# DLRM tower on one core: a first id block laid out per partition, one-hot units of 513 columns for three more steps, a spare lookup bank and a reordered tail

## What is computed

```python
e = jnp.stack([tbl_f[ids[:, f]] for f in range(26)], axis=1)     # (2048, 26, 128)
combined = jnp.concatenate([e, r_dense_x[:, None, :]], axis=1)   # 27 rows a sample
z = jnp.einsum('bfd,bgd->bfg', combined, combined)[:, TRIU_I, TRIU_J]   # 351 pairs
h = jnp.concatenate([z, r_dense_x], axis=1)                      # 479 wide
h = jnp.maximum(h @ W_top1 + b_top1, 0.0)                        # 512
h = jnp.maximum(h @ W_top2 + b_top2, 0.0)                        # 256
y = h @ W_top3                                                   # 1
```

## Time and profile before

| what | us |
|---|---|
| median of 3 runs | 358.75 |
| the profiled execution itself | 359.39 |
| its span, first to last instruction | 357.7 |
| TensorE (PE) busy | 336.0 |
| VectorE (DVE) busy | 238.4 |
| GpSimd (POOL) busy | 250.0 |
| ScalarE (ACT) busy | 178.3 |
| TensorE not busy in the last stretch, 320 to 358 | 7.6 (38.0 less 30.4 busy) |

### The profile page before, as it was taken

How to read it: one execution, slowest core, us unless ns; L and a number is a source line. 1 busy time by engine, 2 the same in 40 slices (tenths; PEclk the granted TensorE clock), 3 DMA queues, 4 the chain that set the end, 5 groups by cost and what they waited for, 6 DMA issues and landing times.

```text
span 357.7 us, 12506 instructions
## 1 busy us (share of the span) xinstructions
PE 336.0 (94%) x5576; PEld 278.2 (78%) x5576; DVE 238.4 (67%) x440; ACT 178.3 (50%) x238; POOL 250.0 (70%) x265
## 2 busy tenths in 40 slices
PE   7998899797999999999999999999999999998976
PEld 7787777676878788877888788787888788977864
DVE  2999989774378856787468784787587793430322
ACT  3898534381617634283535735176344827363412
POOL 6788777777777777777777777777777777777000
PEclk9999999998999999999999999999999999999999
DMA  6988683333343343335253334333443322222000
GB/s 222 369 238 268 171 245 87 87 82 99 71 111 84 86 99 100 85 81 118 64 121 96 82 99 93 88 83 88 100 97 88 94 55 56 66 54 55 24 2 3
DMA packets 19657, 37.67 MB, mean 105 GB/s; under 512 B 5557, under 2 KB 8501, under 8 KB 19604
## 3 DMA queue, kind: packets, MB, share of 16 engines
q1 hardware_dynamic: 11412, 20.09, 20.0%
q0 software_dynamic: 8192, 16.79, 18.6%
HBM read 36.85 MB, written 0.01 MB: 103 GB/s over the span
## 4 chain that ended last, share of the span: by engine, by line
PE 72%; DVE 19%; issue 4%; ACT 2%; DMA 2%; SPq 0%; DVEq 0%; ACTq 0%
PE ps_lk L638 26%; DVE onehot L336 15%; PE ps_gram L664 14%; PE ps_tr L649 8%; PE ps_zt L691 7%; PE ps_mlp L691 6%; PE ps_zt L698 3%; PE ps_mlp L698 3%; DVE table L347 3%; PE ps_lk L711 2%; DMA ids<-in_ids_onehot 2%; PE ps_zt L678 1%; PE ps_lk L726 1%; ACT ids L440 0%; ACT xt L460 0%
## 5 line engine op out<-in xcount | busy, mean ns | idle before, releaser
L294 POOL DMA_INDIRECT rows<-in_tbl,gather_ids x256 | 248.7, 971 | 79.7 <-issue 76.2
L336 DVE TENSOR_SCALAR onehot<-ids 128x513 fp32r<-128x513 f32 (+3 forms) x328 | 179.9, 621 | 40.1 <-PE ps_lk L638 24.0
L638 PE MATMUL ps_lk<-onehot,table 128*128 128x512 f32 (+1 forms) x720 | 160.8, 375 | 4.5 <-DVE onehot L336 1.8
L638 PEld LDWEIGHTS ps_lk<-onehot,table 128*128 128x128 f32 x720 | 121.2, 188 | 29.7 <-DVE onehot L336 3.7
L469 ACT COPY xt<-ps_tr 128x512 f32<-128x512 f32 x64 | 77.2, 1207 | 98.5 <-PE ps_tr L649 98.5
L664 PEld LDWEIGHTS ps_gram<-xt 128*26 128x26 f32 x4096 | 44.1, 103 | 24.5 <-issue 22.6
L664 PE MATMUL ps_gram<-xt 128*26 128x26 f32 x4096 | 53.4, 192 | 9.7 <-issue 6.3
L355 DVE STREAM_TRANSPOSE zs<-ps_gram 128x832 f32<-128x832 f32 x16 | 16.8, 1050 | 62.4 <-PE ps_gram L664 62.4
L448 ACT COPY xt<-ps_lk 128x512 f32<-128x512 f32 x32 | 38.5, 1244 | 9.2 <-PE ps_lk L638 5.2
L649 PE MATMUL ps_tr<-ident,rows 128*128 128x128 f32 x256 | 40.3, 280 | 1.1 <-DMA rows<-in_tbl,gather_ids 0.8
L649 PEld LDWEIGHTS ps_tr<-ident,rows 128*128 128x128 f32 x256 | 30.0, 142 | 7.5 <-issue 1.6
(11 more groups left out here) (62 smaller groups left out, 142.3 us busy)
## 6 DMA issues: line engine op xcount, KB each, us to landing
ids<-in_ids_onehot SPq DMA_DIRECT2D x41, 258.0 KB, 3.7
rows<-in_tbl,gather_ids POOLq DMA_INDIRECT x256
w<-in_tbl SPq DMA_DIRECT2D x6, 512.0 KB, 8.8
h<-in_tbl SPq DMA_DIRECT2D x2, 512.0 KB, 6.8
zt<-in_tbl SPq DMA_DIRECT2D x2, 512.0 KB, 6.5
dense_x<-in_dense SPq DMA_DIRECT2D x8, 128.0 KB
zt<-in_dense SPq DMA_DIRECT2D x8, 128.0 KB, 2.5
w<-in_w SPq DMA_DIRECT2D x1, 512.0 KB
```

The source lines that it names most:

```text
L294: pool.indirect_dma_start(rows[n % ROW_BUFS][:, r, :], None, t_[f"tbl_{GATHERED[r]}"], bass.IndirectOffsetOnAxis(ap=gather_ids[:, n, r:r + ...
L336: nc.vector.tensor_scalar(to, of.bitcast(F32), float(k), None, ALU.is_equal).then_inc(s_unit, 1)
L638: m = nc.tensor.matmul(ps_lk[e % LB][:, x], table[:, i, part, k, :], onehot[:, k, x], start=(k == 0 and j == 0 and part == 0), stop=(k == ...
```

## The change

- Step 0's ids come from a new array that holds one copy for each partition, instead of one row read 128 times.
- `in_thirds(e)`: steps 5, 6 and 7 also use units in three pieces, of 513, 513 and 258 columns.
- Step 11 uses the bank ps_mlp (`SPARE`), and later steps take the three lookup banks with the count shifted by one. Lookup 11 and turn(2,1) stand ahead of gram(1,1). `row_constants` writes its unused product to `packed[1]` instead of ps_mlp and `pack(1)` follows the units of step 12.
- Chunk 1's order on TensorE and ScalarE is changed to match; turn(0,3) stands behind lookup 5.
- Waits ahead of one instruction are put in another order in `lookup` and `turn`; `gram` no longer waits for the lookups of its chunk (other than tile 0), `layer1` does, ahead of its last row block.
- The warm-up has 18 matmuls of 96 columns.
- In the last chunk turn(15,3) stands behind last1(0,2), gram(15,0) and gram(15,1) behind last1(0,3), next to each other, and last2(0) is split in halves around turn_pairs(15).

```diff
+def in_thirds(e):
+    return e >= STEP0[1] - len(BY_CHUNK)
 def cols_of(e):
-    if c == 0:
+    if not in_thirds(e):
         return list(range(n))
-WARM_UP = 20
+WARM_UP = 18
+        SPARE = STEP0[1] + LB
+        def lookup_bank(e):
+            return ps_mlp if e == SPARE else ps_lk[(e if e < SPARE else e - 1) % LB]
-            load_ids(0)
+            sp.dma_start(ids[0][:, :], t_["ids_first"]).then_inc(s_ids[0], 16)
 # VectorE
-                    if STEPS[e][0] == 0:
+                    if not in_thirds(e):
                         to, of = onehot[:, k, 0:w], ids[e % IDS][:, 0:w]
-                nc.vector.tensor_tensor_reduce(ps_mlp[:, 0:H2], bias2[:, :], ...
+                nc.vector.tensor_tensor_reduce(packed[1][...][:, 0:H2], bias2[:, :], ...
             row_constants()
-            pack(1)
             for c in range(1, CHUNKS - 1):
                 make_units(STEP0[c] + 4)
+                if c == 1:
+                    pack(1)
                 make_units(STEP0[c + 1])
 # ScalarE, chunk 1
             evac_new(STEP0[1] + 2)
+            shift(STEP0[1] + 4)
             evac_zt(0)
             evac_group(2, 0)
+            evac_group(2, 1)
...
                 if c == 1:
                     evac_old(e)
-                    shift(e + 4)
                     evac_old(e + 1)
+                    evac_group(a, 2)
+                    shift(e + 5)
+                    evac_old(e + 2)
+                    evac(e + 3)
                     evac_zt(a - 1)
-                    evac_group(a, 1)
-                    evac_old(e + 2)
                     evac_dense(c)
+                    evac_group(a, 3)
+                    evac(e + 4)
+                    relu1(c - 1, 0)
 # TensorE
-                    nc.tensor.matmul(ps_zt[:, 0:P], ident[:, :], ident[:, :], start=True, stop=True)
+                    nc.tensor.matmul(ps_zt[:, 0:3 * Q], ident[:, :], ident[:, 0:3 * Q], start=True, stop=True)
             def turn(n, g):
+                pe.wait_ge(s_rows[n % ROW_BUFS][g], ...)
                 if n * NGR + g > 0:
                     pe.wait_ge(s_turned, n * NGR + g)
-                pe.wait_ge(s_rows[n % ROW_BUFS][g], ...)
             def gram(n, part):
                 if part == 0:
-                    pe.wait_ge(s_lk, STEP0[n // CT + 1])
                     pe.wait_ge(s_turned, (n + 1) * NGR)
+                    if n == 0:
+                        pe.wait_ge(s_lk, STEP0[1])
             turn_pairs(0)
             turn(2, 0)
+            lookup(e + 3)
+            turn(2, 1)
             gram(1, 1)
                 if c == 1:
                     turn(a, 2)
+                    lookup(e + 4)
+                    turn_pairs(a - 1)
+                    turn(a, 3)
+                    lookup(f)
                     pe.wait_ge(s_cols, 16)
                     pe.wait_ge(s_base, 2)
                     pe.wait_ge(s_w, 16 * 4)
+                    pe.wait_ge(s_lk, SPARE + 1)
+                    layer1(c - 1, 0)
                     gram(a, 0)
 # the last chunk on TensorE
             turn_pairs(a)
-            turn(a + 1, 3)
             last1(0, 0)
             last1(0, 1)
+            last1(0, 2)
+            turn(a + 1, 3)
+            last1(0, 3)
             gram(a + 1, 0)
-            last1(0, 2)
-            last1(0, 3)
             gram(a + 1, 1)
-            last2(0, (0, 1, 2))
             for j in range(LB):
                 dense_rows(1, j, True)
+            last2(0, (0, 1))
             turn_pairs(a + 1)
-            last2(0, (3,))
+            last2(0, (2, 3))
 # host side
+    arrays["ids_first"] = np.repeat(arrays["ids_onehot"][0:1], P, axis=0)
```

More of the change, by code:

```diff
@@ L447, in evac @@
                 if w == XT:
-                    nc.scalar.copy(xt[:, :, a], ps_lk[e % LB][:, :]).then_inc(s_lk, 1)
+                    nc.scalar.copy(xt[:, :, a], lookup_bank(e)[:, :]).then_inc(s_lk, 1)
                 else:
@@ L451, in evac @@
                     nc.scalar.copy(xt[:, s:s + CS, a:a + f].rearrange("p s f -> p f s"),
-                                   ps_lk[e % LB][:, 0:f * CS].rearrange("p (f s) -> p f s", f=f)).then_inc(s_lk, 1)
+                                   lookup_bank(e)[:, 0:f * CS].rearrange("p (f s) -> p f s", f=f)).then_inc(s_lk, 1)
             def evac_new(e):
                 act.wait_ge(s_unit_used, (e + 1) * KT // USE)
-                nc.scalar.copy(xt[:, CS:N, NG + 1 + STEPS[e][2][0]], ps_lk[e % LB][:, CS:N])
+                nc.scalar.copy(xt[:, CS:N, NG + 1 + STEPS[e][2][0]], lookup_bank(e)[:, CS:N])
             def evac_old(e):
-                nc.scalar.copy(xt[:, 0:CS, NG + 1 + STEPS[e][2][0]], ps_lk[e % LB][:, 0:CS]).then_inc(s_lk, 1)
+                nc.scalar.copy(xt[:, 0:CS, NG + 1 + STEPS[e][2][0]], lookup_bank(e)[:, 0:CS]).then_inc(s_lk, 1)
             def evac_dense(m):
@@ L521, in _ @@
             evac(5)
+            evac_group(0, 3)
             shift(8)
@@ L633, in lookup @@
                         pe.wait_ge(s_unit, e * KT + k + KT // 2)
+                    if e == 0 and k % (KT // FIRST_PARTS) == 0:
+                        pe.wait_ge(s_low, k // (KT // FIRST_PARTS) + 1)
+                    if 0 < e < STEP0[1] and k == 0:
+                        pe.wait_ge(s_low, split_count(tables[-1]))
+                    if e >= LB and e != SPARE and k == 0:
+                        pe.wait_ge(s_lk, e - LB if SPARE < e <= SPARE + LB else e - LB + 1)
                     for j, i in enumerate(tables):
@@ L636, in lookup @@
                         for part in range(2):
-                            m = nc.tensor.matmul(ps_lk[e % LB][:, x], table[:, i, part, k, :], onehot[:, k, x],
+                            m = nc.tensor.matmul(lookup_bank(e)[:, x], table[:, i, part, k, :], onehot[:, k, x],
                                                  start=(k == 0 and j == 0 and part == 0),
@@ L690, in layer1 @@
                     r = ZT[k][1] if k < NZ else D
+                    if j == 0 and k == NZ:
+                        pe.wait_ge(s_lk, STEP0[m + 2])
                     i = nc.tensor.matmul(mlp_bank(j)[:, 0:CS], w1[0:r, k, j * P:(j + 1) * P], zt[0:r, k, :],
@@ L718, in dense_rows @@
             def dense_rows(t, j, first):
+                if first:
+                    pe.wait_ge(s_act, last_act(t - 1) + j + 1)
                 return nc.tensor.matmul(last1_bank(t, j), w1[:, NZ, j * P:(j + 1) * P], zt[:, NZ, t * P:(t + 1) * P],
@@ L741, in _ @@
             lookup(4)
+            lookup(5)
             turn(0, 3)
-            lookup(5)
             lookup(6)
@@ L764, in _ @@
                 a, e, f = c * CT, STEP0[c], STEP0[c + 1]
-                if c > 1:
-                    turn(a, 3)
-                lookup(e + 3)
-                turn_pairs(a - 1)
-                if c == 1:
-                    turn(a, 1)
-                lookup(e + 4)
                 if c == 1:
                     turn(a, 2)
+                    lookup(e + 4)
+                    turn_pairs(a - 1)
+                    turn(a, 3)
+                    lookup(f)
                     pe.wait_ge(s_cols, 16)
@@ L776, in _ @@
                     pe.wait_ge(s_w, 16 * 4)
-                layer1(c - 1, 0)
-                if c == 1:
-                    turn(a, 3)
-                    lookup(f)
+                    pe.wait_ge(s_lk, SPARE + 1)
+                    layer1(c - 1, 0)
                     gram(a, 0)
                 else:
+                    turn(a, 3)
+                    lookup(e + 3)
+                    turn_pairs(a - 1)
+                    lookup(e + 4)
+                    layer1(c - 1, 0)
                     gram(a, 0)
```

15 lines of the change are left out of this document (4 added, 11 removed).

## The result

The changed kernel takes 360.53 us (median of 20 runs, 358.57 to 362.88), the kernel before 358.49 in the same comparison: the ratio is 1.0052 (95% interval 1.0033 to 1.0071), 2.0 us slower. A second comparison of the same kernel gave 360.33 against 359.04, 1.0029 (1.0003 to 1.0056). The forecast was 357.2, with 354.6 to 360.6 as its range.

What follows compares the result with a forecast made beforehand. VectorE paces TensorE up to 47 us, then TensorE bounds itself, with GpSimd's gathers just behind. +0.1 - 1.1 - 1.4 + 0.4 + 0.5 = -1.5 us on the profiled 359.39, 357.2 in terms of the runs; range 354.6 to 360.6.

Steps and rivals of the forecast that it cites:

- the ids and `low_first`: Start of VectorE's chain: ids at about 3.9, low_first from 8.91 to about 6.2; -2.7 us.
- the length of the longer units: Steps 5 to 7 on VectorE: eight units take 4.85 us instead of 2.87; together +5.3 us.
- the pauses of gram(1,1) and gram(2,0): TensorE's fetch pauses: gram(1,1)'s 1.40 us goes; of gram(2,0)'s 2.24 half comes back, -1.1, and its slow clock, -1.4.
- A microsecond of VectorE is a microsecond of the kernel: Start up to 47 us: VectorE paces TensorE, so its gains and losses pass fully into the kernel's time.
- 0.8 us earlier: GpSimd in steps 5 to 7: about six gathers beside the new units are relieved of 0.14 us each.
- GpSimd's cap at turn(4,3) allows 2 to 3 us of lead there: Chunks 2 to 6: gathered rows leave TensorE room for more than the 2.4 us of lead taken.
- The s_lk wait moved to layer1 cost nothing while the copies are done: Wait for the chunk's lookups, with the order of waits: no cost, bounds ±0.5 us.
- Chunks 2 to 6 are unchanged: Middle of the kernel: these chunks were taken as unchanged, with no term of their own.
- The first rival: Fetch pauses stay in new places, gram(2,0) and the adjacent parts of gram(15): 360.8 us, chance 0.20.
- Its added clause, a slow clock in chunk 0: Part of the pauses-stay rival: if the clock falls in waits before lookups 6 and 8, lookup 8 costs 1.4 us more.
- two terms: Tail: gram(14,0)'s pause of 1.19 grows by some 0.4; the last chunk's new order costs +0.5, bounds -1.7 and +1.5.
- The terms for the pauses: Work ahead of a block border decides: 2.2 us back in gram(1,1), +0.4 in gram(14,0), +0.5 in the tail.

Runs made afterwards that it cites:

- second profile: The profiled execution of after_again, the changed kernel unedited: 361.87 us.
- after_plain_units: Changed kernel with steps 5 to 7 back to contiguous units, all else kept: 358.59 us, ratio 0.9987.
- before_shift_back16: Kernel before with a warm-up of 67 tiny and 13 full matmuls, putting the gram(8,0) border where the changed kernel has it: 359.06 us, 1.0002.
- after_shift16: Changed kernel with 4 tiny extra matmuls (16 instructions) ahead of lookup 8: 362.41 us, ratio 1.0081.
- after_again: Changed kernel once more, unedited, for a second profile: 360.33 us, ratio 1.0029.
- after_wait_back: Changed kernel with the wait for the chunk's lookups put back ahead of gram: 360.48 us, ratio 1.0042.
- before_wait_early: Kernel before with the wait for the lookups added in layer1's first block, its waits ahead of gram kept: 360.35 us, ratio 1.0055.
- before_thirds: Kernel before with only steps 5, 6 and 7 in units of 513, 513 and 258 columns: 362.33 us, ratio 1.0070.

## Why the prediction was wrong

**Right, within 0.3 us:** the ids and `low_first`; the length of the longer units; lookup 11 without a wait and lookup 12 with one of 0.34; the pauses of gram(1,1) and gram(2,0) and the slow clock of 80 to 90 gone. That is why turn(3,0) starts at 85.96 in the changed kernel, as before (85.98), although lookup 8 ended 4 us later, and why TensorE takes 25.2 us from there until it is ready for turn(4,3), instead of 26.9. It was ready at 112.56 - 1.43 = 111.13, 1.7 us ahead of before.

**Lookup 8 ended 1.4 us later than forecast** (51.1, forecast 49.7). "A microsecond of VectorE is a microsecond of the kernel" did not hold for the ids: of the 2.6 us won at VectorE's first unit 0.75 are left at step 5, since TensorE waits for the rows of turn(0,0) until 13.3 and then frees the units later than VectorE wants them. TensorE was then ready for turn(4,3) with a lead of 1.7 us instead of the forecast 2.4.

**The step that failed first: "GpSimd's cap at turn(4,3) allows 2 to 3 us of lead there".** It allowed 0.3, and none in the second profile. The reading of the kernel before was not far off. Its last gather of the group ends at 109.38 and the rows have landed at 110.96 (from the times of their semaphore in the trace), 1.6 us later, so that the turn at 112.86 stood 1.9 us behind them. Two things took this away. First, GpSimd did not come 0.8 us earlier but 0.44 later (109.82): its first gather starts 0.2 later, and of the gathers beside `low` one took 2.98 us, beside two of these operations in a row (before 1.89), while those beside the new units saved 0.14 each as read. Second, the rows took 2.7 us to land:

```profile
108.88 3.64 DMA rows<-in_tbl,gather_ids
112.52 0.04 issue
112.56 0.66 PE ps_tr L661 x4
```

The reason is the lead itself. VectorE ends a step's units earlier, and with them comes the load of a later step's ids, 258 KB on SyncE's queue. Its issue in the changed kernel, in the kernel before, and in `after_plain_units`:

```profile
108.44 0.33 SPq L237 DMA_DIRECT2D ids<-in_ids_onehot  x1
110.35 0.33 SPq L228 DMA_DIRECT2D ids<-in_ids_onehot  x1
104.75 0.33 SPq L237 DMA_DIRECT2D ids<-in_ids_onehot  x1
```

In the changed kernel it moves its bytes from 109.5 to 111.6, when the gathered rows are to land. The DMA queues from the gather's end to the landing, 109.8 to 112.5, where q1 is SyncE's queue (packets, MB, share):

```profile
q1 hardware_dynamic: 121, 0.22, 36.7%
q0 software_dynamic: 71, 0.14, 20.6%
```

Before, 109.4 to 111.0, the rows have the engines to themselves:

```profile
q0 software_dynamic: 32, 0.07, 18.6%
```

The load ran from 111.7 there, behind the rows, and from 105.9 to 108.0 in `after_plain_units`, ahead of them; in that kernel this group's rows landed 1.7 us behind the gather, and turn(4,3) had a lead of 2.4 us, the cap that was forecast. At this turn the rows landed 2.3 to 2.7 us behind the gather in the seven profiles that have the load beside them, and 1.4 to 1.9 us in nine of the other ten; the tenth (`before_shift_back16`) has 2.7 without it, so other causes exist. Over all turn groups from tile 2 on, in the 17 traces, the median is 1.6 us without this load and 2.75 beside it.

So the sum at this turn is 1.9 of slack, less 0.44 for the later gather, less 1.1 for the later landing: 0.3. Of the forecast lead of 2.4, 1.4 went into the wait. This turn also stands on a block border in the changed kernel. The kernels shifted by 16 and 64 instructions have the border elsewhere and still start it 2.44 to 2.49 us after the gather's end (`after_shift16`: 110.97 and 113.46, with a wait of 1.49), and the contiguous ones 1.6 to 1.7 with the border there or elsewhere. So it is the rows, and the border adds 0.3 at most. The cap also cuts the other way: `after_plain_units` reaches turn(1,1) 4.6 us earlier and keeps only 2.1 of them, and with gathers left out the units cost 4.5 us. So the ids, the spare bank and the two vanished pauses together could not give more than the cap, whatever they saved in chunks 0 to 2.

**"The s_lk wait moved to layer1 cost nothing while the copies are done".** The condition was stated and not looked up. The copy of a lookup takes 1.18 us on ScalarE and starts behind the lookup's last matmul; layer1's last row block comes sooner. That is 1.2 us in the rows. What it costs in time is not shown: putting the wait back gave nothing.

**"Chunks 2 to 6 are unchanged".** Their order is, their block borders are not: WARM_UP and the waits moved them by some instructions. A pause of 1.6 to 2.05 us in gram(8,0) stands in the profiles of `after_again`, `after_plain_units`, both kernels with fewer gathers and `after_wait_back`, though not in the first one of the changed kernel. In all, it stands in five of the eight profiles with the border where the changed kernel has it, in one of seven (`before_wait_early`, 1.95 us) with the border where the kernel before has it, and in neither of the two with it elsewhere. From turn(8,3) to turn(9,0) `after_again` takes 19.5 us, the first profile 16.3. This is most of what separates these two executions; that the typical run of the changed kernel (+2.0) is slower than the profiled one (-0.6) for the same reason is likely and not shown, since the timed runs have no trace. The first rival, pauses that stay in new places with 360.8, named the mechanism and nearly the time, but not the place: it put them in gram(2,0) and gram(15,1), which ran through. That its 360.8 is close to 360.53 is luck. Its added clause, a slow clock in chunk 0, held in four of the eight profiles with long units (`after_again`, `before_thirds`, `after_shift16`, `after_wait_back`) and in none of the contiguous ones before 50; turn(1,1) then starts about 1.25 us later, which the cap takes in again.

**The tail** was forecast 0.9 slower in two terms and came out 1.0 faster (turn(14,0) to the end: 47.4 before, 46.4 after): the pauses of 1.19 in gram(14,0) and of 1.48 in gram(15,1) were gone, and last2 had one of 1.37. This hid, in the profiled execution, most of what the cap took.

**The terms for the pauses** (2.2 us back in gram(1,1), 0.4 more in gram(14,0), 0.5 in the tail) were set by how much work lies ahead of a border. No run shows a length of work that decides, nor the last two terms: the first came back as forecast, and in place of the other two both pauses were gone. What the runs show is the place: each pause over 0.9 us that no semaphore explains stands where the count is 192 or 193 over a multiple of 256, in all kernels, if the separate wait instructions are counted with the matmuls and their loads. But most borders pass without one, and a pause of gram(8,0) comes and goes between two executions of one program. The Trainium skill's "Runtime: NRT & Kernel Launch" (Instruction fetch mechanics) calls the crossing of a block "mostly hidden"; by these traces that holds for most of the 44 and fails, with 0.9 to 2.7 us, mostly where gram lies on the border. What decides between the two is open.

The sum of the changed kernel by its own profile: -0.3 at turn(4,3), +0.5 from there to turn(14,0) (the moved wait, less two short pauses of before), -1.0 in the tail, so -0.8, where -1.5 was forecast. For `after_again` the pause in gram(8,0) makes the middle +3.0. The times alone say this: the units cost 1.7 to 1.9, and the rest of the change gave nothing.

## What to carry to other kernels

Before a lead is booked, read the second bound at its tightest place, from the end of the *landing* and not of the instruction that issues it, and ask which transfers the lead itself will move onto that landing: a microsecond on the pacing engine is worth a microsecond only up to there. A wait that moves ahead of work is free only if what it waits for is done at the new place: look up the length of that copy. And where a long program without loops has dense small matmuls, an edit of a few instructions moves all the borders behind it, and kernels that differ by little else came out up to 2 us apart here; test an edit at two alignments, in timed rounds, before believing a gain or a loss of that size.

## What the hardware showed beyond that

A gram part of 128 small matmuls takes 1.82 us while gathers run and 1.27 us while none starts; 14 gathers less make the kernel 4.5 us faster, with contiguous units 7.2. The difference is not a slower rate. In the traces it is made of stalls of 0.1 to 0.35 us between two matmuls. Of 815 such stalls, in the gram parts without a pause of 17 profiles, 802 end 0.10 to 0.20 or 0.55 to 0.70 us after a gather instruction of GpSimd has started, at any instruction count. A part in which no gather starts takes 1.27 us also where 32 packets of gathered rows move during it. So it goes with GpSimd's instruction, not with the landing of the rows or the fetch of a block. Of the gram parts ahead of the last tile, seven take 1.27 us in each kernel with fewer gathers, one and three in the two profiles of the changed kernel, and two in `after_plain_units`. At 0.55 us each that makes, as an estimate, 2 to 3 us of what leaving out gathers gave. The Trainium skill's "SBUF — State Buffer" (Who interferes with whom) gives TensorE ports of its own and has DMA never contend with a compute engine. For the landing rows the trace agrees (1.27); for the gather instructions the rows differ (1.82), and the measurement decides. What the stall is stays open. The last gathers end between 324 and 335 in all kernels, and the tail's gram parts take 1.2 us.

Gathers beside VectorE's two-input `low` operations took 1.84 to 2.98 us, beside contiguous units 1.09, alone 0.94.

The pause in gram(8,0) was followed by a clock of 0.83 in `after_again` (1.62 us), and by one of 1.00 in `after_plain_units` (2.05 us): the length of a pause alone does not say whether the clock falls.
